# Adding the LayerNorm beta on GpSimd, half by half, instead of by an accumulating DMA

## The reference

```
q = emb @ Wq + bq;  k = latent @ Wk + bk;  v = latent @ Wv + bv
w = softmax((q k^T) / sqrt(E), over the 224 query rows)
x = w @ v + emb
out = (x - mean) * rsqrt(var + 1e-6) * gamma + beta      # per row of 512
```

## Time and profile before

| | |
|---|---|
| median of 3 runs | 1169.45 us (1168.15 to 1172.15) |
| the profiled execution | 1172.15 us |
| its span, first to last instruction | 1170.3 us |
| mean granted TensorE clock | 0.968 |
| busy: PE, DVE, ACT, POOL | 92%, 78%, 67%, 60% |
| DMA queue of GpSimd | 28.91 MB, 16.5% of the 16 engines' span |
| DMA queue of SP | 59.71 MB, 16.0% |

### The profile page before, as it was taken

One profiled execution on the slowest core, in us unless ns is written; L12 is line 12 of the kernel. 1 busy time (PEld: TensorE's weight loads), 2 busy tenths in 40 slices (PEclk: granted clock), 3 DMA queues, 4 the chain that ended last, 5 costly groups with the idle time before them and its releaser, 6 DMA issues.

```text
span 1170.3 us, 26382 instructions
## 1 busy us (share of the span) xinstructions
PE 1073.8 (92%) x8392; PEld 997.5 (85%) x8392; DVE 918.2 (78%) x2561; ACT 780.3 (67%) x2033; POOL 707.6 (60%) x583
## 2 busy tenths in 40 slices
PE   7999999999999999999989999999998999999983
PEld 7889888888898888889888888988898988888873
DVE  3468879877888778887878788887887878888864
ACT  2457766766776666776676677667766766766642
POOL 0244666666566557666666766765676566667643
PEclk9889999999999899999999999999999999999996
DMA  8122322333332233332223333322333322333222
GB/s 211 72 59 59 86 56 57 77 84 89 89 79 62 46 79 89 89 88 59 57 67 85 89 89 89 73 47 63 84 89 89 83 63 54 74 81 90 49 48 47
DMA packets 34338, 89.05 MB, mean 76 GB/s; under 512 B 5072, under 2 KB 7120, under 8 KB 34304
## 3 DMA queue, kind: packets, MB, share of 16 engines
q0 software_dynamic: 15120, 28.91, 16.5%
q1 hardware_dynamic: 16544, 59.71, 16.0%
q10 hardware_dynamic: 2640, 0.01, 0.2%
HBM read 45.03 MB, written 14.68 MB: 51 GB/s over the span
## 4 chain that ended last, share of the span: by engine, by line
DMA 43%; PE 29%; ACT 10%; issue 7%; DVE 4%; POOL 4%; SPq 3%; ACTq 0%; POOLq 0%; DVEq 0%
DMA raw<-in_ctx_dram 28%; DMA y_out<-beta_row 14%; PE score_bank L545 4%; PE score_bank L547 4%; PE score_bank L546 4%; POOL y_out L1208 3%; PE t_bank L472 3%; ACT probs L759 3%; ACT probs L750 3%; PE oq_bank L562 3%; PE oq_bank L564 3%; PE oq_bank L563 3%; ACT z L793 2%; PE t_bank L490 1%; SPq L350 1%
## 5 line engine op out<-in xcount | busy, mean ns | idle before, releaser
L1191 POOL TENSOR_TENSOR rstd<-ve,minus_half 112x1 f32<-112x1 f32 x128 | 122.4, 956 | 177.2 <-DVE ve L1032 175.8
L545 PE MATMUL score_bank<-qT_hi,cT_hi 128*125 128x224 f32 x768 | 225.6, 294 | 3.5 <-DVE qT_lo L946 1.7
L562 PE MATMUL oq_bank<-pr_hi,cn_hi 125*128 125x224 f32 x768 | 213.9, 279 | 14.2 <-DVE pr_lo L977 12.5
L750 ACT ACTIVATE probs<-scores,neg_max 125x224 f32<-125x224 f32 x384 | 179.8, 471 | 52.4 <-DVE neg_max L962 52.2
L546 PE MATMUL score_bank<-qT_lo,cT_hi 128*125 128x224 f32 x768 | 214.3, 279 | 0.0
L547 PE MATMUL score_bank<-qT_hi,cT_lo 128*125 128x224 f32 x768 | 214.1, 279 | 0.0
L563 PE MATMUL oq_bank<-pr_lo,cn_hi 125*128 125x224 f32 x768 | 213.0, 277 | 0.0
L564 PE MATMUL oq_bank<-pr_hi,cn_lo 125*128 125x224 f32 x768 | 213.0, 277 | 0.0
L962 DVE CUSTOM_DVE_ANT_0 scores<-score_bank,d_row 125x224 f32<-125x224 f32 x384 | 132.9, 383 | 91.6 <-PE score_bank L547 91.0
L793 ACT ACTIVATE z<-y,nmr,rstd 112x512 f32<-112x512 f32 x128 | 104.3, 815 | 126.1 <-DVE nmr L1039 126.0
L1169 POOL TENSOR_TENSOR cn_lo<-raw,cn_hi 125x768 fp32r<-125x768 f32 x64 | 130.6, 2042 | 89.8 <-DMA beta_row<-in_L_xattn_beta_dram 47.8
(11 more groups left out here) (106 smaller groups left out, 2906.1 us busy)
## 6 DMA issues: line engine op xcount, KB each, us to landing
raw<-in_ctx_dram SPq DMA_DIRECT2D x32, 750.0 KB
x<-in_x_dram SPq DMA_DIRECT2D x32, 448.0 KB, 4.8
x<-beta_row POOLq DMA_DIRECT2D x32, 448.0 KB, 9.5
y_out<-beta_row POOLq DMA_DIRECT2D x31, 448.0 KB, 5.7
out_dram<-y_out SPq DMA_DIRECT2D x31, 448.0 KB, 3.3
y<-in_L_xattn_Wq_dram SPq DMA_DIRECT2D x4, 512.0 KB, 11.0
x<-in_L_xattn_Wk_dram SPq DMA_DIRECT2D x2, 512.0 KB, 9.9
x<-in_L_xattn_Wv_dram SPq DMA_DIRECT2D x2, 512.0 KB, 11.0
```

Of the source, the lines that this page charges most:

```text
L545: nc.tensor.matmul(o, hi, qT_hi[:, l, :], start=(l == 0), stop=False)
L562: nc.tensor.matmul(o, hi, pr_hi[0:MP, u.par, c, :], start=(c == 0), stop=False)
L750: ins = act.activation(probs[0:MP, u.par, c, :], scores[0:MP, c, :], ACT.Exp, bias=neg_max[0:MP, c:c + 1], scale=-1.0, accum_out=ssum[0:MP ...
```

## The change

Beta is added by GpSimd instructions, one per half, in place of the DMA. `add_beta(u, h)` waits for that half's scale and adds `beta_row` in place. There is one semaphore `ln_done` for all halves in place of the four `beta_added`. The adds have places of their own in GpSimd's list. For `prev` (layer 0, tile `x1`) half 0 follows the two scales, and half 1 stands after `inverse_deviation(last, 0)`. For `last` (layer 1, tile `y_out`) each half's add follows its scale. VectorE's lists and SP's order are as before, apart from the semaphore that they wait on.

```diff
 # SyncE, odd slots
-                    sp.wait_ge(beta_added[1][done.slot], done.turns(16))
+                    sp.wait_ge(ln_done, done.n(m=2))
                     sp.sem_inc(wait_alone, 1)
                     sp.dma_start(out[...], y_out[0:TP, done.slot]).then_inc(stored[done.slot], 16)
 # VectorE, residual
                 if u.layer and h == 0:
-                    dve.wait_ge(beta_added[0][u.slot], u.turns(16))
+                    dve.wait_ge(ln_done, u.n(-UNIT_GAP, 2))
 # GpSimd
-            def add_beta(u):
-                ...
-                pool.wait_ge(zg_done, u.n(m=2))
-                pool.sem_inc(wait_alone, 1)
-                pool.dma_start((x1, y_out)[u.layer][0:TP, u.slot], beta_row[0:TP, u.layer, :].unsqueeze(1).to_broadcast([TP, TH, E]),
-                               accum_op=ALU.add).then_inc(beta_added[u.layer][u.slot], 16)
+            def add_beta(u, h):
+                if not u.real:
+                    return
+                if u.j is None and u.u == LAST and h == 1:
+                    return
+                pool.wait_ge(zg_done, u.n(m=2, add=h - 1))
+                o = (x1, y_out)[u.layer][0:TP, u.slot, h, :]
+                pool.tensor_tensor(o, o, beta_row[0:TP, u.layer, :], ALU.add).then_inc(ln_done, 1)
 # GpSimd, even slots
                     scale(prev, 0)
                     scale(prev, 1)
-                    add_beta(prev)
+                    add_beta(prev, 0)
                     ctx_lo(now, 0)
                     inverse_deviation(last, 0)
+                    add_beta(prev, 1)
                     ctx_lo(now, 1)
                     sum_probs(now)
                     inverse_deviation(last, 1)
                     scale(last, 0)
+                    add_beta(last, 0)
                     scale(last, 1)
-                    add_beta(last)
+                    add_beta(last, 1)
                     inverse_deviation(now, 0)
```

More of the change, by code:

```diff
@@ L267, in build_xattn @@
         zg_done = sem("zg_done")
-        beta_added = [[sem("beta_added00"), sem("beta_added01")], [sem("beta_added10"), sem("beta_added11")]]
+        ln_done = sem("ln_done")
         last_zg_done = sem("last_zg_done")
-        last_ln_done = [sem("last_ln_done0"), sem("last_ln_done1")]
+        last_ln_done = sem("last_ln_done")
         wait_alone = sem("wait_alone")
@@ L342, in slot @@
                     rows = out[done.batch()].rearrange("(p h) e -> p h e", h=TH)
-                    for h in range(TH):
-                        sp.wait_ge(last_ln_done[h], 1)
-                        sp.dma_start(rows[:, h, :], y_out[0:TP, done.slot, h, :]).then_inc((stored[done.slot], last_stored)[h], 16)
+                    sp.wait_ge(ln_done, done.n(m=2, add=-1))
+                    sp.dma_start(rows[:, 0, :], y_out[0:TP, done.slot, 0, :]).then_inc(stored[done.slot], 16)
+                    sp.wait_ge(last_ln_done, 1)
+                    sp.dma_start(rows[:, 1, :], y_out[0:TP, done.slot, 1, :]).then_inc(last_stored, 16)
                 elif done.real:
-                    sp.wait_ge(beta_added[1][done.slot], done.turns(16))
+                    sp.wait_ge(ln_done, done.n(m=2))
                     sp.sem_inc(wait_alone, 1)
@@ L1049, in finish @@
                 dve.wait_ge(last_zg_done, 1)
-                dve.tensor_tensor(o, o, beta_row[0:TP, u.layer, :], ALU.add).then_inc(last_ln_done[h], 1)
+                dve.tensor_tensor(o, o, beta_row[0:TP, u.layer, :], ALU.add).then_inc(last_ln_done, 1)
             u0 = Unit(0)
```

## The result

The changed kernel takes 1182.87 us (median of 4 runs, 1181.1 to 1185.1); the kernel before took 1170.35 us (1168.15 to 1172.15) beside it. The forecast had the sign and not the size: 1235 us were predicted, +65.5, and +12.5 came. The range (1160 to 1265) holds it, and it is the first rival's time (1170 to 1186).

The account below looks back on a forecast made before the run. VectorE was taken to be late next once the late context load, behind SP's store, is in time. 33.58 + 1.30 + 0.96 + 0.66 = 36.50 us a period, +65.5 us over 29 periods: 1235 us, range 1160 to 1265.

Parts of the forecast that it names:

- the first rival: VectorE gets in at GpSimd's first boundary, pr_lo ends at 117.6; period 34.8 or 34.2 us, 1170 to 1186; chance 0.15.
- The context wait: TensorE's 2.0 us wait at line 472 goes as beta's DMA goes; gain at most 0.66 us a period.
- `add_beta(prev, 0)`: GpSimd's add after the scales of x, over before the next residual; costed at nothing, 1.30 us if not covered.
- `add_beta(prev, 1)`: Between rstd and cn_lo; pr_lo stands through three instructions, TensorE waits at line 562; +1.30 us, bounds -0.94 and +1.63.
- `add_beta(last, 0)`: y_out half 0's add runs as dot comes; dot ends late and delays oT_lo, for which TensorE waits; +0.73 us.
- `add_beta(last, 1)`: y_out half 1's add delays the second pr_lo and score_max; 0.96 us for the last two adds, bounds 0 and 1.9.
- The half-clock stretches: Difference between the mean period and the full-clock one, kept at 0.66 us a period; bounds 0 and 1.3.

Follow-up runs that it names:

- the run with x1 adds and a cleared head: Changed kernel with x1 half-1 add and cn_lo ahead of inverse_deviation(last, 0), y_out's beta by DMA, loads ahead of the store; 1133.13 us, 0.9744.
- the kernel with the x half-1 add early: Changed kernel with add_beta(prev, 1) moved right behind add_beta(prev, 0), ahead of ctx_lo(now, 0); 1248.73 us, ratio 1.0728.
- the run with all adds moved: Changed kernel with add_beta(prev, 1) right behind add_beta(prev, 0) and both y_out adds behind both y_out scales; 1236.6 us, ratio 1.0622.

## Why the prediction was wrong

*The context wait* was right. There is no wait at the context transposes, and taking it away alone gave 0.6 us a period between the profiled executions and 0.35 by the medians (0.66 forecast as the bound).

*`add_beta(prev, 0)`* at nothing: right, as far as the run with x1 adds and a cleared head shows (32.9 against 32.95); no run takes this add alone out of the changed kernel.

*`add_beta(prev, 1)`*, the failed step, and the largest term (+1.30). I wrote that `pr_lo` "now stands through three instructions and ends 1.30 us later", TensorE's wait going from 0.94 to 2.24. I had the case in which VectorE gets in as a bound of -0.94 and took the other end, because at 116 us it had not got in. In every regular period it did: 1.14 us, no wait of TensorE. The run without this add shows that the add is what opened the way (3.27 us without it, and a slower kernel). The cost went to GpSimd's side instead, where I had priced nothing in the forecast: the second `rstd` late, `nmr` +1.38 us, `psum_all` +0.47. Rival 1 had named this path, with the scale in the add's place before `dot`, and its 34.2 to 34.8 us hold both the 34.4 and the mean of 34.66.

*`add_beta(last, 0)`*, +0.73 through `dot` and `oT_lo`: the wait grew by 0.85, but not by this add. (The 124.94 isn't consistent with my own rule: 0.74 us behind 124.32 is 125.06, and +0.85; the measured ends of `dot` lie about 0.55 us behind GpSimd's, 229.12 behind 228.58 in the run with the x half-1 add left out.) With the second `rstd` late, `dot` stands behind the scale, with or without an add behind it. Only with a head as before does my mechanism show, with +0.64 us.

*`add_beta(last, 1)`*: I let `residual` through first and charged +0.23 more, for 0.96 with the one before, at the second `pr_lo`. That `pr_lo` takes 1.87 us as before and TensorE doesn't wait for it. Where the y_out adds do cost, it is `residual` that stands (1.77) and +0.65 at line 523; in the changed kernel the second `residual` takes 0.81.

*The half-clock stretches*: kept at 0.66 because TensorE's waits would stay about as long; measured 34.66 - 34.40 = 0.26. They don't go by the sum of the waits: the kernel with the x half-1 add early waits longest (period 36.8) and has none in its regular periods. What brings them on stays open.

The terms were added as if independent. They aren't: the two y_out adds cost 1.6 us a period with a punctual second `rstd`, and no more than their DMA with a late one. The nearest to the forecast's 36.5 is the kernel with the x half-1 add early (36.8), where each collision has a wait of its own.

## What to carry over

Where one engine has to stand while another reads, an instruction put into the other's list also moves the boundaries at which the first can get in; it may free the neighbour while it delays its own engine. Price such an edit for both engines, once with the neighbour getting in and once not, and don't add up the collisions behind it: here the first lateness decided which of the later ones still happened. Where an engine waits just ahead of a crowded stretch (here 3.50 us before `rstd`), move work that is already ready into that wait.

## What was not expected of the hardware

Whether VectorE gets in at a boundary of two back-to-back GpSimd instructions isn't decided by the instructions or by when VectorE became ready, as far as the traces resolve it. In the run with all adds moved, at the same boundary (add, `rstd`) and with the same 0.34 us between `pr_lo`'s start and `rstd`'s, VectorE doesn't get in at 133 us and does at 207 us: in the first two regular periods not, in the 26 behind them always. The first two take 37.2 us, the others 36.3. GpSimd and VectorE, once and again:

```profile
133.30 0.55 POOL L1192 TENSOR_TENSOR rstd<-ve,minus_half 112x1 f32<-112x1 f32 x1
133.82 1.64 POOL L1178 TENSOR_TENSOR psum<-probs 125x672 f32<-125x672 f32 x1
...
207.66 1.16 POOL L1192 TENSOR_TENSOR rstd<-ve,minus_half 112x1 f32<-112x1 f32 x1
```
```profile
132.96 3.21 DVE L978 TENSOR_TENSOR pr_lo<-probs,pr_hi 125x672 fp32r<-125x672 f32 x1
...
207.32 1.09 DVE L978 TENSOR_TENSOR pr_lo<-probs,pr_hi 125x672 fp32r<-125x672 f32 x1
```

In the other kernels the outcome at one place was the same in all regular periods: not behind `cn_lo` with the sum or the add next (ahead of the regular periods VectorE did get in there, at 84.04 us in the kernel before), always behind the x1 add, always behind `cn_lo` with `rstd` next. The Trainium skill, "SBUF — State Buffer", section "Who interferes with whom", says that whoever issues first has the shared pair for the whole instruction while the other blocks. The 1.14 us agree with it if the stand ends with that instruction. The 3.2 us don't: there VectorE stood through the end of `cn_lo` and all of the sum, or, at 133 us, through the end of the add, `rstd` and the sum. What decides is open.
